# V's product one score later in the attention loop of a hybrid transformer block

## The reference

```python
q, k, v = (_split(lora_linear(layernorm(x), W, b, B, A)) for each of q, k, v)
scores = jnp.einsum('bhqd,bhkd->bhqk', q, k) * SCALE
attn = jax.nn.softmax(scores, axis=-1)
out = jnp.einsum('bhqk,bhkd->bhqd', attn, v)
...
x = x + lora_linear(out, Wo, bo, Bo, Ao)
x = x + ffn(layernorm(x))          # ternary weights, gelu
x = x + attn_b(layernorm(x))       # attention over the heads of one token
x = x + ffn(layernorm(x))
```

## Time and profile before

| | |
|---|---|
| median of 3 runs | 415.2 us (414.1 to 416.36) |
| the profiled execution's own time | 415.58 us |
| its span, from first to last instruction | 413.4 us |
| busy PE / DVE / ACT / POOL | 89% / 75% / 60% / 36% |
| granted TensorE clock, mean | 0.955 |
| units 0 to 6 of the attention | about 58 to 220 us |
| unit 7 and the later blocks | about 220 us to the end |

### The profile page before, as it was taken

The page is one execution under the profiler, slowest core; times in us unless marked ns, Lnnn a source line. Parts: engine busy times, 40 slices in busy tenths (PEclk is TensorE's granted clock), DMA queues, the critical chain, the costliest instruction groups (busy, mean ns, idle before and its releaser), DMA issues.

```text
span 413.4 us, 6021 instructions
## 1 busy us (share of the span) xinstructions
PE 366.8 (89%) x2157; PEld 167.5 (41%) x2157; DVE 308.2 (75%) x501; ACT 249.9 (60%) x433; POOL 150.4 (36%) x169
## 2 busy tenths in 40 slices
PE   7998889989999999989989997988889598977696
PEld 4544421212221222222123435775665365544485
DVE  7469987988888887978852354685898879999543
ACT  2672137888888898888989665233443363562331
POOL 4050189960000000000000013354877768947143
PEclk9999957999999999999999999999899789899799
DMA  7768723534000000000000000000000000000001
GB/s 195 252 116 132 186 39 61 106 70 88 2 0 2 0 2 0 2 0 2 1 1 2 2 0 0 2 2 0 2 1 2 0 0 2 25 1 2 25 2 51
DMA packets 14672, 14.22 MB, mean 34 GB/s; under 512 B 5235, under 2 KB 12979, under 8 KB 14454
## 3 DMA queue, kind: packets, MB, share of 16 engines
q1 hardware_dynamic: 12214, 11.70, 12.6%
q10 hardware_dynamic: 2176, 1.64, 1.3%
q0 software_dynamic: 256, 0.52, 0.8%
HBM read 5.40 MB, written 1.06 MB: 16 GB/s over the span
## 4 chain that ended last, share of the span: by engine, by line
PE 58%; DVE 21%; ACT 13%; issue 4%; DMA 1%; POOL 1%; ACTq 1%; DVEq 0%
PE ps L1354 16%; PE ps L1340 11%; ACT pbuf L869 10%; PE ps L1494 6%; PE ps L1483 4%; DVE mx L1051 4%; PE ps L1317 4%; DVE s_wide L1152 4%; PE ps L1269 3%; DVE xn L980 3%; PE ps L1468 3%; DVE pack L1141 2%; PE ps L1529 2%; DVE stats L963 2%; PE ps L1258 1%
## 5 line engine op out<-in xcount | busy, mean ns | idle before, releaser
L869 ACT ACTIVATE pbuf<-ps,exp_scale 128x512 f32<-128x512 f32 x256 | 158.3, 691 | 31.5 <-PE ps L1340 31.1
L1051 DVE TENSOR_REDUCE mx<-ps 128x1 f32<-128x1024 f32 x128 | 150.9, 1220 | 24.9 <-PE ps L1317 24.3
L1340 PE MATMUL ps<-pack 64*128 64x512 f16 x256 | 88.8, 391 | 7.8 <-ACT pbuf L869 1.3
L1354 PE MATMUL ps<-pbuf,v_slot 128*32 128x512 f32 x512 | 69.1, 611 | 5.1 <-ACT parts L854 3.2
L1340 PEld LDWEIGHTS ps<-pack 64*128 64x128 f16 x256 | 19.9, 94 | 97.3 <-issue 52.6
L1317 PE MATMUL ps<-pack 64*128 64x512 f16 x128 | 50.1, 395 | 4.6 <-DVE mx L1051 4.2
L1494 PE MATMUL ps<-w_nat,pack 128*128 128x256 bf16 x384 | 52.3, 280 | 1.7 <-POOL pack L719 1.6
L731 POOL TENSOR_TENSOR pbuf<-wT 128x1024 f32<-128x1024 f32 (+3 forms) x32 | 49.9, 1573 | 8.5 <-ACT wT L920 8.5
L1317 PE MATMUL ps<-parts,pack 64*128 64x512 f16 x128 | 51.2, 404 | 0.0
L694 POOL COPY v_slot<-v_sb 128x512 f32<-128x512 f32 x8 | 4.9, 613 | 127.3 <-PE ps L1354 105.9
L719 POOL TENSOR_TENSOR pack<-pack 128x256 bf16<-128x256 f32 x64 | 42.1, 668 | 24.7 <-DVE pack L1141 24.7
(11 more groups left out here) (136 smaller groups left out, 393.8 us busy)
## 6 DMA issues: line engine op xcount, KB each, us to landing
w_nat<-in_L_ffn_w_dram SPq DMA_DIRECT2D x2, 1024.0 KB, 8.2
pack<-pack SPq DMA_DIRECT2D x3, 512.0 KB, 4.8
pack<-pbuf SPq DMA_DIRECT2D x20, 64.0 KB, 2.8
x_res<-in_L_attn_a_x_dram SPq DMA_DIRECT2D x4, 256.0 KB, 3.7
pack<-parts SPq DMA_DIRECT2D x16, 64.0 KB, 2.3
pack<-parts SPq DMA_DIRECT2D x32, 32.0 KB, 2.0
out_dram<-x_res SPq DMA_DIRECT2D x4, 256.0 KB, 2.1
w_nat<-in_L_attn_b_Wqkv_dram ACTq DMA_DIRECT2D x1, 768.0 KB, 5.2
```

The source lines that it names most:

```text
L869: act.activation(pbuf[:, c % 2, j, :], ps[:, b, :], ACT.Exp, scale=exp_scale[:, 0:1]).then_inc(drained[b], 1)
L1051: dve.tensor_reduce(mx[:, par, k:k + 1], ps[:, b:b + 2, :].rearrange("p b k -> p (b k)"), AX_X, ALU.max) \
L1340: pe.matmul(ps[:, b, :], k_group[0:ROWS, at, j, P * c:P * c + P].rearrange("p g t -> p (g t)"), q_rows[0:ROWS, at, qh, j, :].rearrange("p ...
L1354: ins = pe.matmul(ps[32 * j:32 * j + 32, PV_BANK, :], v_slot[:, qh, c, j, :], pbuf[:, c % 2, j, :], start=(c == 0), stop=(c == TT - 1))
```

## The change

V's product of chunk c stands behind score 4c + 6 of its unit, where it stood behind score 4c + 5. To keep the program otherwise the same, `unit()` counts s from 3 to 34 and V's product comes at s % 4 == 2; three scores of the first unit are issued between the lead tiles (k = 3, 4, 5), and each unit issues three scores of the next one. LEAD stays 7. ACT, DVE, POOL and SP have the same instructions in the same order.

```diff
@@ last_unit_slots
-    for s in range(2, STEPS):
+    for s in range(3, STEPS):
         yield LAST_STEP * s, ("score", s)
@@ the lead tiles
-                if k == LEAD - 3:
+                if k == LEAD - 4:
                     pe.wait_ge(far_keys_packed, 16 * G)
                     pe.wait_ge(shift_landed, 16)
-                if k >= LEAD - 3 and k < LEAD - 1:
-                    score_tile(0, 0, 0, k - (LEAD - 3))
+                if k >= LEAD - 4 and k < LEAD - 1:
+                    score_tile(0, 0, 0, k - (LEAD - 4))
@@ unit()
-                for s in range(2, STEPS + 2):
+                for s in range(3, STEPS + 3):
...
-                    if s % G == 1 and s > G:
+                    if s % G == 2 and s > G:
                         times_v(qh, u, s // G - 1)
```

## The result

The changed kernel took 400.35 us (median, 398.8 to 402.43) beside 414.65 us for the kernel before: ratio 0.966, 95% interval 0.960 to 0.971. Two later sets of runs of the same code gave 401.6 us (ratio 0.968, 0.962 to 0.973) and 401.46 us (0.967, 0.964 to 0.971). The forecast was 399.0 with a range of 396 to 404.

The account below looks back on a forecast made before the run. It took a loop of ACT and PE waiting for each other, neither full, as the bound. Savings of 14.7 (units 1 to 6) and 1.8 (unit 0) made 16.5 us, from 415.2 to 398.7, stated as 399.0; range 396.0 to 404.0.

Parts of the forecast that it names:

- The loop in mid-unit: ACT and PE waiting for each other within a unit: a chunk falls from 2.74 to 2.47 us.
- The drain of the tiling mode: Rival: V's product starts 0.39 us behind the score ahead, not 0.32; chunk 2.54, 402.5 us in all; chance 0.15.
- The shift: The chunk with the transpose takes 2.63 us, 0.16 over a normal one; split maxima ready some 0.1 us early.
- the gap ahead of the transpose: Sign of being wrong: PE shows a gap before line 1331 that is put down to DVE; no size given.
- The end of a unit: Two chunks around ACT's copy take 5.23 us where two normal ones take 4.94, 0.29 more.
- A unit: A whole unit takes 20.21 us against 22.66 before, saving 2.45, counted for units 1 to 6.
- Unit 6: Counted as the last of six equal units, 1 to 6, each saving 2.45 us, 14.7 together.
- Unit 0: First unit: saves 1.8 us, 1.6 from six chunks and 0.2 from an earlier start; bounds 1.3 and 2.9.
- Unit 7: Last unit, product already behind the third score; one score moves ahead at its start, costed at nothing, ±0.3 us.
- The SP queue: Shift DMA of unit 2 moves from 100.21 to about 96.5 us; its score, needing it at about 101, holds.
- Behind it: Work after unit 7 moves up as a block; low-clock slices of the later blocks may fall otherwise, ±1.5 us.
- the rival with one exposed matmul: One second matmul of a max tile per chunk no longer hides: chunk 2.61 us, about 408 us; chance 0.04.

Follow-up runs that it names:

- the fourth: Changed kernel with V's product behind the fourth score, four scores ahead, max tiles at even steps and the shift at step 24: 402.92 us, ratio 0.970.
- the longest set: Changed kernel again without an edit, with more runs, beside a version that copies on DVE: 401.46 us, ratio 0.967 against the kernel before.
- The repeat: Changed kernel run again without an edit, for a second trace of the later blocks: 401.6 us, ratio 0.968 against the kernel before.

## Why the prediction was right, step by step

- **The loop in mid-unit**: 2.47 forecast, 2.48 measured. ACT's wait is 0.18, forecast 0.16. The 0.32 beside which the forecast set it is another measure, the idle time from the end of the exponential ahead; by that one it is now 0.06 (148.29 + 0.74 = 149.03 to 149.09), and by the other it was 0.44. Its single links hold (score to product 0.31 to 0.32, product to score 1.00, the wait ahead of the third score), and the experiments confirm it from both sides: a slot on it costs 0.21 to 0.22, a slot beside it 0.13, one place less costs one exponential.
- **The drain of the tiling mode** (the rival at 0.39): the earlier trace rows were the better guide. The step costs 0.31 to 0.32 in the loop too, 0.10 over the 0.22 of two scores, and as much in the fourth (134.77 to 135.09), where the product's own exponential has long ended. The Trainium skill, "TensorEngine Tiling (Array Packing)", Tiling Modes, says that changing the mode drains the engine; the 0.10 agrees with a drain much shorter than the whole score. No run separates it from the step from f16 to f32 at the same place.
- **The shift**: 2.63 forecast, 2.64. The split maxima come 0.11 before they are needed, as reckoned. In unit 0 they can be late: in the longest set's trace the chunk with the shift took 3.57 us there, with the gap ahead of the transpose that the forecast named as a sign of being wrong:

```profile
75.51 1.12 DVE L1058 TENSOR_SCALAR m_parts<-mx 128x16 f16<-128x16 f32 x1
...
76.89 0.23 PE L1331 MATMUL ps<-identh,m_parts 128*128 128x128 f16 x1 [0.82 <-DVE m_parts L1060]
```

DVE's first cut took 1.12 us and not 0.17. It ended at 76.63, 0.03 behind an instruction of POOL (line 708, 75.44 to 76.60); whether that held it is not shown. In six of the other traces a gap of 0.17 to 0.65 us stood at the same place of unit 0, in one of them (0.39) with the product behind the second score, so it does not come with the new place alone. No trace has it in another unit.
- **The end of a unit**: 5.23 forecast, 5.27.
- **A unit**: 20.21 forecast, 20.32; it saves 2.34 and not 2.45, the sum of the hundredths above, the 0.01 eight times among them.
- **Unit 6**: mis-sized. It was counted as one of six equal units, and the ±0.3 for the work that begins there stood at unit 7. It saves 2.08, 0.37 less than its term, 0.26 less than the five ahead of it. Its eight products are spaced as in the others; what is longer is the way from the last of them to the copy, 2.56 us for 2.01 (before: 2.88 for 2.58). The first transposes of the weights (line 1427) stand between that product and the fourth score of unit 7:

```profile
203.35 1.07 PE L1354 MATMUL ps<-pbuf,v_slot 128*32 128x512 f32 x8
204.35 0.62 PE L1427 MATMUL ps<-identb,tern 128*128 128x128 bf16 x8
204.91 0.60 PE L1340 MATMUL ps<-pack 64*128 64x512 f16 x2
```

Their 0.56 us (204.35 to 204.91) are the 0.55 by which that way is longer. Before, ACT still had the third score's exponential to do when the fourth score was late, and only 0.30 showed; now the fourth score is the one that ACT waits for, and all of it shows. Units 1 to 6 give 13.8 for the 14.7 forecast.
- **Unit 0**: 1.8 forecast, with bounds of 1.3 and 2.9; 2.8 in the first pair of traces, 0.6 and 0.7 with the later traces of the same code. The part that belongs to the order came out: from the second V's product (67.03 before) to the copy it took 19.19 us before and 17.14 in the first two traces after. Of these 2.05 us, six chunks are 1.49 (1.6 forecast) and 0.57 is the copy, now 2.01 behind the last product and not 2.58, which the forecast had left out for this unit. The start is not settled: the second product began at 67.03 us before and at 66.31, 68.47 and 67.57 in the three traces after. In the window from 48 to 72 us the granted clock was 0.72 before, 0.86 in the first trace after and 0.72 in the second; but with 0.72 on both sides the unit saves 0.6, and with 0.86 on both (the run behind the second score, 85.50) 2.1, so the clock's share alone does not account for it. That 2.8 lay within the bounds was luck.
- **Unit 7**: nothing, as forecast, where the clock is the same.
- **The SP queue**: the shift DMA of unit 2 was forecast at about 96.5 us and was issued at 96.25, behind the group's last copy at 95.59; neither held a score up.
- **Behind it**: no term in the sum, only ±1.5. It took 1.6 back in the profiled execution. The forecast named it as a sign of being wrong if unit 7 and the later blocks got longer. From the copy of unit 6 to the end they took 190.9 us before and 192.5, 189.7 and 192.3 in the three traces after: longer in two of them. The repeat shows that the order did not do it, since the same code is both longer and shorter than before; what moves it is the low clock. The spread over the traces behind unit 7, 4.7 us for the same code, is larger than all the errors of the attention part together.

The sum of measured terms is 2.8 + 13.8 + 0.0 - 1.6 = 15.0, against 16.5. The mechanism was right. What was off is what the forecast took for fixed outside the loop, the start of unit 0, the end of unit 6 and the clock at both ends, and the 0.1 us a unit of rounded links. Partly they cancel: unit 0 gave 1.0 more than its term in this trace and the other units 0.9 less. One sum of the forecast does not come out, that of the rival with one exposed matmul: 415.2 - (0.13 x 56 - 1) is 408.9 and not about 408; nothing rests on it.

## What to carry to other kernels

Where two engines wait for each other once a period, write the loop as a list of links with a duration from a row each, and move instructions until the sum is smaller; here that gave the new period to 0.01 us from the trace before. Moving a consumer one place later takes one stage of the pipeline off the loop, but adds whatever now stands directly ahead of it, so keep that to one slot and do not expect the next place to gain again. When the median moves by less than the sum says, compare the traces in stages first: a part with unchanged code differed here by 2.7 us between two traces through the granted clock alone.

## What the runs showed of the hardware

- A matmul on rows 64 to 127 starts ahead of one on rows 0 to 63 that precedes it in the program: 148.68 beside the score at 148.67, while its partner, issued before it, starts at 148.90. DVE's maximum still starts only at 149.32, behind the end of that partner (149.28). Thus records of PE do not always start in the order of the program, though what waits for them keeps to it, and the second matmul of a max tile cost no slot wherever it stood in these orders.
- A score directly followed by V's product takes 0.31 to 0.32 us of PE and not 0.22, at 2.4 GHz (149.84 to 150.15, 134.77 to 135.09).
- An ACT instruction with two waits started 0.50 us behind the matmul that it waited for where ACT's code is a loop with wait values from a register, and 0.42 to 0.43 where the code is written out with constants (units 1 to 5 and unit 6 of the fourth). With one wait it was 0.42 in both.
- The same code behind unit 7 took 161.1 us with the clock low for 7 us near 310 us, and 163.9 with it low for 14. In the longest set's trace the clock fell to 1.2 GHz at 234 us after four microseconds with PE busy for 3.03 of them; in the first trace it stayed at 2.4 GHz behind the same work with 2.89 of 4 busy.
